# Every fourth product with B of a chunked scan moves from VectorE to GpSimd, and the carry copies from GpSimd to ScalarE

## The reference

```python
def step(h, t):
    dt_t, B_t, C_t, u_t = t
    h = h * jnp.exp(dt_t[:, :, None] * A) + (dt_t * u_t)[:, :, None] * B_t[:, None, :]
    y = jnp.einsum('bds,bs->bd', h, C_t)
    return (h, y)
```

## Time and profile before

| | |
|---|---|
| median of 3 runs | 1236.7 us (1234.82 to 1236.95) |
| the profiled execution | 1233.87 us, its span 1232.1 us |
| PE busy in the span | 891.5 us (72%) |
| VectorE busy | 875.3 us (71%) |
| ScalarE busy | 471.2 us (38%) |
| GpSimd busy | 465.3 us (38%) |
| scan stage | about 574 to 1125 us of the span |

### The profile page before, as it was taken

How to read it: one execution, slowest core, us unless ns; L and a number is a source line. 1 busy time by engine, 2 the same in 40 slices (tenths; PEclk the granted TensorE clock), 3 DMA queues, 4 the chain that set the end, 5 groups by cost and what they waited for, 6 DMA issues and landing times.

```text
span 1232.1 us, 10624 instructions
## 1 busy us (share of the span) xinstructions
PE 891.5 (72%) x3525; PEld 399.4 (32%) x3525; DVE 875.3 (71%) x1130; ACT 471.2 (38%) x846; POOL 465.3 (38%) x389
## 2 busy tenths in 40 slices
PE   4784066577757999855767776777777777778787
PEld 3342034556625665532111111111111111113366
DVE  0134989865542222147999999999999999996466
ACT  0255140174352444647333333333333333333641
POOL 0002557620100000000667666666666656663100
PEclk9897587686576999987666656655655655567988
DMA  9800000700100000001110110110110110100001
GB/s 230 143 0 0 0 1 0 149 2 1 52 1 0 1 1 1 1 11 27 37 30 8 37 38 7 31 37 8 30 37 8 30 37 10 28 1 0 1 10 29
DMA packets 28244, 33.03 MB, mean 27 GB/s; under 512 B 10142, under 2 KB 27550, under 8 KB 27678
## 3 DMA queue, kind: packets, MB, share of 16 engines
q1 hardware_dynamic: 28190, 32.36, 11.7%
HBM read 17.57 MB, written 1.20 MB: 15 GB/s over the span
## 4 chain that ended last, share of the span: by engine, by line
DVE 37%; PE 36%; issue 13%; ACT 7%; POOL 3%; SPq 2%; DMA 2%; DVEq 0%; POOLq 0%; ACTq 0%
DVE pair_arrays L1474 14%; DVE pair_arrays L1460 9%; PE PS L563 3%; PE PS L718 3%; PE PS L572 3%; PE PS L700 2%; PE PS L588 2%; ACT pair_arrays L861 2%; POOL pair_arrays L1189 2%; PE PS L499 2%; DMA big<-in_x 2%; PE PS L690 2%; PE PS L806 2%; DVE pair_arrays L1294 2%; PE PS L470 2%
## 5 line engine op out<-in xcount | busy, mean ns | idle before, releaser
L1189 POOL TENSOR_TENSOR pair_arrays<-pair_arrays 128x736 f32<-128x736 f32 x192 | 338.1, 1761 | 65.5 <-DVE pair_arrays L1474 65.5
L861 ACT ACTIVATE PS<-PS,A_negative 128x368 f32<-128x368 f32 x384 | 191.5, 537 | 350.2 <-PE PS L700 350.2
L1474 DVE TENSOR_TENSOR_SCAN pair_arrays<-PS,scan_carry,pair_arrays 128x368 f32<-128x368 f32 x256 | 239.2, 973 | 0.0
L1460 DVE TENSOR_TENSOR pair_arrays<-pair_arrays,PS 128x736 f32<-128x736 f32 x192 | 172.9, 901 | 8.6 <-PE PS L690 8.4
L1186 POOL COPY scan_carry<-pair_arrays 128x2 f32<-128x2 f32 x128 | 26.9, 210 | 314.6 <-DVE pair_arrays L1474 314.6
L718 PE MATMUL PS<-pair_arrays,weights 128*32 128x368 f32 x768 | 131.8, 764 | 2.2 <-POOL pair_arrays L1189 2.1
L690 PE MATMUL PS<-spread_rows,token_weights 96*128 96x368 bf16 x192 | 70.8, 466 | 75.5 <-DVE pair_arrays L1460 69.8
L1148 POOL TENSOR_TENSOR big<-pair_arrays 128x1104 f32<-128x1104 f32 (+15 forms) x32 | 60.7, 1915 | 150.1 <-DVE pair_arrays L1248 114.4
L690 PE MATMUL PS<-pair_arrays,token_weights 96*128 96x368 bf16 x192 | 72.7, 477 | 56.7 <-DVE pair_arrays L1460 56.7
L1474 DVE TENSOR_TENSOR_SCAN pair_arrays<-PS,pair_arrays 128x368 f32<-128x368 f32 x128 | 111.6, 909 | 0.0
L470 PE MATMUL PS<-big,weights 128*128 128x368 f32 (+15 forms) x192 | 57.3, 462 | 34.5 <-DVE big L1305 23.6
(11 more groups left out here) (191 smaller groups left out, 1363.0 us busy)
## 6 DMA issues: line engine op xcount, KB each, us to landing
big<-in_x SPq DMA_DIRECT2D x8, 1024.0 KB, 21.1
big<-decay_rows SPq DMA_DIRECT2D x4, 1104.0 KB, 15.3
spread_rows<-pair_arrays SPq DMA_DIRECT2D x96, 46.0 KB, 1.9
pair_arrays<-pair_arrays SPq DMA_DIRECT2D x96, 46.0 KB, 1.9
spread_rows<-big SPq DMA_DIRECT2D x48, 46.0 KB, 1.9
pair_arrays<-big SPq DMA_DIRECT2D x48, 46.0 KB, 1.9
weights<-in_wts SPq DMA_DIRECT2D x1, 2204.0 KB, 20.2
big<-in_wexp SPq DMA_DIRECT2D x1, 1536.0 KB, 7.5
```

The lines of the kernel that those rows point to most:

```text
L861: return nc.scalar.activation(o, i, fn, **kw)
L1189: nc.gpsimd.tensor_tensor(hcbuf[t % NRING], hbuf[t % NRING], c4(seg).unsqueeze(1).to_broadcast([128, 2, G]), ALU.mult).then_inc(s("hc_read ...
L1460: tt(bx[t % NRING], b4(seg).unsqueeze(1).to_broadcast([128, 2, G]), PS[:, 2:4, 0:G], ALU.mult).then_inc(s("b_used"), 1)
L1474: nc.vector.tensor_tensor_scan(hbuf[t % NRING][:, h, :], PS[:, 4 + 2 * (t % 2) + h, 0:G], bx[t % NRING][:, h, :], carry[:, a:a + 1] if k e ...
```

## The change

GpSimd takes the product with B of each step with t mod 4 = 3 (shared(t)), 48 of the 192. ScalarE copies the spread input of such a step out of banks 2 and 3 (move_input, 128x736) into a part of the tile token_weights (moved), and GpSimd multiplies from there. The input of step t + 4 is spread at step t, at the place at which that of t stood: the order of the spreads is 3, 0, 1, 2 within four. PE's spread_input waits for x_moved where the one before was a shared step's, and otherwise for VectorE's own products, counted by own_to. ScalarE copies at step t ahead of decay(t). GpSimd's input_term(t + 3) stands ahead of output_term(t) for t mod 4 = 0. The carry copies go from GpSimd to ScalarE, carry_on(t - 1) behind decay(t), and VectorE waits for the carried count of four steps back. The stack of a block is waited for at the spread of its step 3, which is now issued first.

```diff
@@ -192,6 +192,18 @@
                              (P1.rearrange("p a t -> p (a t)")[:, 0:NJ * G], P10.rearrange("p a t -> p (a t)")[:, 0:NJ * G]))]
         rest = [[m.rearrange("p a t -> p (a t)")[:, (NJ + i) * G:(NJ + i + 1) * G] for i in range(2)] for m in (P1, P10)]
 
+        moved = Wt[:, 1024:1024 + 2 * G].rearrange("p (h t) -> p h t", h=2)
+        order = (3, 0, 1, 2)
+
+        def shared(t):
+            return t % 4 == 3
+
+        def inputs_to(t):
+            return t - t % 4 + order.index(t % 4) + 1
+
+        def own_to(t):
+            return t + 1 - (t + 1) // 4
+
         def high(a):
             return a.bitcast(BF16).rearrange("p (t two) -> p t two", two=2)[:, :, 1]
 
@@ -215,6 +227,7 @@
         hbuf, hcbuf, bx = ring(0), ring(1), ring(2)
         carry = sb("scan_carry", [128, B * DS])
 
+        CARRIED = (NG - 1) * B * NSTEP
         STACKED = 16 * 2 * 3 * NJ
 
         def at(i, seg):
@@ -682,10 +695,14 @@
             def spread_input(t):
 
                 seg, i = t // NSTEP, t % NSTEP
-                if i == 0:
+                if i == 3:
                     pe.wait_ge(s(f"stack_in{seg % 2}"), STACKED * (seg // 2 + 1))
-                if t:
-                    pe.wait_ge(s("b_used"), t)
+                if t % 4 == 0:
+                    pe.wait_ge(s("x_moved"), t // 4 + 1)
+                elif t % 4 < 3:
+                    pe.wait_ge(s("b_used"), own_to(t - 1))
+                elif t > 3:
+                    pe.wait_ge(s("b_used"), own_to(t - 5))
                 for h in range(2):
                     last = nc.tensor.matmul(PS[:, 2 + h, 0:G], pick[:, (i // 2) * 128:(i // 2 + 1) * 128],
                                             high(stack[seg % 2][1][0:3 * DB, 2 * (i % 2) + h]), start=True, stop=True)
@@ -720,8 +737,12 @@
                                             skip_group_check=True)
                 last.then_inc(s("y_added"), 1)
 
+            spread_input(3)
             for t in range(NSEG * NSTEP):
-                spread_input(t)
+                if not shared(t):
+                    spread_input(t)
+                elif t + 4 < NSEG * NSTEP:
+                    spread_input(t + 4)
                 spread_step(t)
                 if t % 2 == 0 and t >= 4:
                     add_y(t - 4)
@@ -1076,8 +1097,26 @@
                     f(PS[:, bank, 0:G], PS[:, bank, 0:G], ACT.Exp, scale=aneg[:, g:g + 1]).then_inc(s("decay"), 1)
 
             act.wait_ge(s("a_ready"), 1)
+            def move_input(t):
+
+                act.wait_ge(s("x_spread"), inputs_to(t))
+                if t >= 4:
+                    act.wait_ge(s("bx_ready"), t // 4)
+                f(moved, PS[:, 2:4, 0:G], ACT.Copy).then_inc(s("x_moved"), 1)
+
+            def carry_on(t):
+
+                b, i = t // NSTEP % B, t % NSTEP
+                act.wait_ge(s("scanned"), 2 * (t + 1))
+                f(carry[:, b * DS + 2 * i:b * DS + 2 * i + 2], hbuf[t % NRING][:, :, G - 1], ACT.Copy).then_inc(s("carried"), 1)
+
+            move_input(3)
             for t in range(NSEG * NSTEP):
+                if shared(t) and t + 4 < NSEG * NSTEP:
+                    move_input(t + 4)
                 decay(t)
+                if 1 <= t <= CARRIED:
+                    carry_on(t - 1)
             for g in range(NGR + 2):
                 if g < NGR:
                     p, k = groups[g]
@@ -1181,15 +1220,24 @@
 
                 seg, i = t // NSTEP, t % NSTEP
                 pool.wait_ge(s("scanned"), 2 * (t + 1))
-                if seg // B < NG - 1:
-                    a = (seg % B) * DS + 2 * i
-                    nc.gpsimd.tensor_copy(carry[:, a:a + 2], hbuf[t % NRING][:, :, G - 1]).then_inc(s("carried"), 1)
                 if t >= NRING:
                     pool.wait_ge(s("y_added"), t - NRING + 1)
                 nc.gpsimd.tensor_tensor(hcbuf[t % NRING], hbuf[t % NRING], c4(seg).unsqueeze(1).to_broadcast([128, 2, G]),
                                         ALU.mult).then_inc(s("hc_ready"), 1)
 
+            def input_term(t):
+
+                pool.wait_ge(s("x_moved"), t // 4 + 1)
+                if t >= NRING:
+                    pool.wait_ge(s("scanned"), 2 * (t - NRING + 1))
+                nc.gpsimd.tensor_tensor(bx[t % NRING], b4(t // NSTEP).unsqueeze(1).to_broadcast([128, 2, G]), moved,
+                                        ALU.mult).then_inc(s("bx_ready"), 1)
+
+            pool.wait_ge(s("dt_ready"), NG)
+            pool.wait_ge(s("b_ev"), NPAIR * NG)
             for t in range(NSEG * NSTEP):
+                if t % 4 == 0:
+                    input_term(t + 3)
                 output_term(t)
             pool.wait_ge(s("x_spread"), NSTEP * NSEG)
             pool.wait_ge(s("dt_spread"), NSTEP * NSEG)
@@ -1456,7 +1504,7 @@
             def input_term(t):
 
                 seg = t // NSTEP
-                dve.wait_ge(s("x_spread"), t + 1)
+                dve.wait_ge(s("x_spread"), inputs_to(t))
                 tt(bx[t % NRING], b4(seg).unsqueeze(1).to_broadcast([128, 2, G]), PS[:, 2:4, 0:G], ALU.mult).then_inc(s("b_used"), 1)
 
             def scan_half(t, h):
@@ -1464,11 +1512,13 @@
                 seg, i = t // NSTEP, t % NSTEP
                 b, k = seg % B, seg // B
                 if h == 0:
-                    dve.wait_ge(s("b_used"), t + 1)
+                    if shared(t):
+                        dve.wait_ge(s("bx_ready"), t // 4 + 1)
+                    else:
+                        dve.wait_ge(s("b_used"), own_to(t))
                     if t >= NRING:
                         dve.wait_ge(s("hc_ready"), t - NRING + 1)
-                    if k:
-                        dve.wait_ge(s("carried"), t - B * NSTEP + 1)
+                        dve.wait_ge(s("carried"), min(t - NRING + 1, CARRIED))
                 dve.wait_ge(s("decay"), 2 * t + h + 1)
                 a = b * DS + 2 * i + h
                 nc.vector.tensor_tensor_scan(hbuf[t % NRING][:, h, :], PS[:, 4 + 2 * (t % 2) + h, 0:G], bx[t % NRING][:, h, :],
@@ -1482,7 +1532,8 @@
             for t in range(NSEG * NSTEP):
                 if t:
                     scan_half(t - 1, 0)
-                input_term(t)
+                if not shared(t):
+                    input_term(t)
                 if t:
                     scan_half(t - 1, 1)
                 if t % NSTEP == 2 and t // NSTEP < NSEG - 1:
```

## The result

| | before | changed |
|---|---|---|
| median | 1236.8 us (1234.8 to 1238.3, 4 runs) | 1198.9 us (1195.0 to 1201.9, 4 runs) |
| profiled execution (its span) | 1233.9 us (1232.1) | 1200.5 us (1198.7) |
| first scan starts, span begun | 581.95 us | 586.07 us |
| scan stage, first scan to the end of the last | 539.2 us | 505.6 us |
| behind the last scan | 110.9 us | 107.1 us |

The ratio is 0.969 (95% interval 0.966 to 0.973): 38 us, 3.1%, in the medians, and 33.4 us between the two profiled executions. Forecast was 1206.0 us and a gain of 30.7 us on the profiled execution. The median lies 0.9 us above the lower end of the stated range, 1198. The stage itself gave 33.7 us; the stretch ahead of it is 4.1 us longer and the one behind it 3.8 us shorter in these two profiles, which the next run of the same kernel shows to be scatter.

The account below looks back on a forecast made before the run. VectorE was taken to bound the scan stage. Gains of 19.4, 3.7 and 10.9 us make 34.0, less 3.3 at splits is 30.7: 1203.2 us profiled, 1206.0 us median; own range 1198 to 1212, whole range 1198 to 1227.

Parts of the forecast that it names:

- VectorE as the bound, and the products' worth: Scan stage: VectorE always at work; each of 48 products taken off is worth its pitch, 0.81 us, together 38.9 us.
- The decay chain: Shared steps: scan(t,0) waits for its decay, 0.35 us (first part) or 0.13 us (second); none at steps 3 and 7.
- The splits: VectorE's 11 splits wait for GpSimd's output_term(0), 0.2 to 0.4 us each, 3.3 us in all.
- the sign of the port: At the split: VectorE's first instructions at over 1 us would show the forecast wrong in size.
- the port rival: At each split GpSimd's next product also gets in first: another 19 us, 1225 us; chance 0.14.
- GpSimd keeps up: Scan stage: five GpSimd products take 8.75 us per four steps of 9.4 or 9.6 us; lag hidden, 85 to 90% busy.
- The carries: 128 carry copies moved from GpSimd to ScalarE in the scan stage, put under what costs nothing.
- The small copies: ScalarE's 128 copies of 128x2 in the scan stage, costed at 0.2 us each.
- Table loads: On ScalarE: a copy after an exponential brings no table load.
- The start of the stage: Copy and second spread_input delay decay(0) by some 1.6 us, at no cost: ready at 577.6, first scan at 581.95.
- The earlier wait for the stack: The block's stack is wanted one step earlier, at the fifteenth step; costs nothing, its DMAs being issued early enough.
- the upper bound: Scan stage: the gain if no stall gives anything back, 48 products at 0.81 us, 38.9 us.

Follow-up runs that it names:

- decay_first: Changed kernel with ScalarE's copy of the next input behind the shared step's decay instead of ahead of it; 1235.1 us.
- split_at_0: Changed kernel with the split of blocks 2 to 11 at step 0 of the block ahead, block 1's staying at step 2; 1213.5 us, one run.
- gp_twice: Changed kernel with each of GpSimd's 48 products with B made twice; 1241.6 us.
- split_gp_sooner: Changed kernel with start_y at step 1, splits of blocks 2 to 11 on GpSimd and the block's stack ready sooner; 1157.8 us.
- both halves: Changed kernel with carry copies back on GpSimd, 1200.6 us; kernel before with carry copies on ScalarE and all products on VectorE, 1235.1 us.
- after_again: The changed kernel run once more, nothing edited, in five rounds; 1202.1 us.
- carries_only: Kernel before with only the carry copies moved to ScalarE, all 192 products still on VectorE; 1235.1 us.

## Why the prediction was right

- **VectorE as the bound, and the products' worth.** Right. 48 products, each 0.83 us by the table (0.81 forecast): 39.8 against 38.9 us.
- **The decay chain.** Right to 0.02 us where it binds: stalls of 0.37 and 0.13 us against 0.35 and 0.13, in steps 11 and 15 and not in 3 and 7. Some of these steps have none or little, so the sum is 4.2 us against 4.9; why they have none was not taken apart. decay_first showed the same chain from its other side.
- **The splits.** The size was forecast at 3.3 us and is 2.1 us: 0.4 us in blocks 1 to 3, as worked out, but 0.01 to 0.17 us in the others. The step's picture was wrong in one point: VectorE does not keep its turn for both L1489. What the forecast named as the sign of the port, a first instruction of the split at over 1 us, is there in every split (the pair takes 2.5 to 2.8 us), and the 19 us that it was to cost are not: the GpSimd instruction that gets in first is the same one that the second pair waited for before. That was luck of the count, since GpSimd had only one instruction ready while the split ran. With two ready, in split_at_0 and gp_twice, a split costs 1.1 to 2.3 us more than in the changed kernel, and a price like that of the port rival (1.75 us each) is there.
- **GpSimd keeps up.** Right: 1745 to 1756 ns, and waited for only inside the splits. It is at work 82% of the stage and not 85 to 90%. Its condition holds further than I thought (97% at work in split_gp_sooner) and is narrower in another way: its lag is paid wherever VectorE reads two SBUF tiles (gp_twice).
- **What was costed at nothing.** The carries: 0.5 us of stage in both halves. The small copies take 206 ns, as put. Table loads: none in the stage. The start of the stage: decay(0) ends at 583.1, and VectorE is at its earlier work until 585.1. PE does wait for x_moved, 37 times for 10.5 us together, but all that VectorE waits for a spread (8.7 us) is step 4's. The earlier wait for the stack: nothing here, 2.2 to 3.3 us per block once its cover is gone.
- **The forecast of 1206.0 us.** The terms missed by 0.9 (product), 0.7 (stalls) and 1.2 us (splits), all to the same side; they make 2.8 of the 3.0 us by which the stage's 33.7 us are above the forecast 30.7. The other 4 us between 1206.0 and the measured 1198.9 are not the stage's: the runs of one program scatter by 7 us (changed kernel) and 10 us (after_again), with the medians of its two sets at 1198.9 and 1202.1. How near the median came to the lower end of the range is therefore chance; the stage's gain stays 5 us under the upper bound of 38.9.

Left open is what makes the first scan start between 578.5 and 586.7 us with the same program ahead of it. In the two first profiles the input loads of the first stage land later in the changed kernel, but no run took that apart.

## What to carry to other kernels

Where one engine is busy to 98% and its neighbours idle, moving one instruction in four is worth its pitch, and what is given back is found by laying the new order on the rows of the chain that the moved instruction had been hiding. Look for the queue in which the added copy stands: here its place decided between 34 us and 1.6 us of stage. After the move look for the small fixed costs that the bound engine still pays, and at each wait that has been moved forward: those of the split and start_y, with the stack made in time for them, were worth 44 us of stage against the change's 34.

## What the runs showed of the hardware

- A GpSimd product is not stretched by VectorE's scans beside it, nor they by it, at any load that was run: 1746 ns with GpSimd at work 97% of the time, scans with a carry of 955 to 984 ns there and 951 to 996 ns in the kernel before. Of the instructions in this stage only the split's, with two SBUF inputs, and GpSimd's block each other, a whole instruction at a time, and the next turn goes to either of the two that wait (GpSimd 4 times and VectorE 7 times in carries_only).
- TensorE's level behind the stage differs from one execution to the next of the same program: eight passes in 2.74 or 5.28 us. With one program the stretch ahead of the stage differed by 5.9 us and the one behind it by 6.5 us between two profiles, while the stage itself repeated within 0.13 us; so a gain or a loss of that size outside the part that an edit touches can't be put down to the edit.
